# Second attention: q, k and v projections as products of 64 rows in two banks of PSUM

## What is computed

```python
xh = x.reshape(b, c, h, he).transpose(0, 2, 1, 3)         # 16 heads of 16 numbers
qkv = jnp.einsum('bhce,ef->bhcf', xh, Wqkv) + bqkv         # the same 16 x 48 weights for every head
q, k, v = jnp.split(qkv, 3, axis=-1)
att = jnp.einsum('bhqe,bhke->bhqk', q, k) / jnp.sqrt(jnp.float32(he))
mask = jnp.tril(jnp.ones((c, c), dtype=att.dtype), k=-1)
att = jax.nn.softmax(att * mask, axis=-1)
out = jnp.einsum('bhqk,bhke->bhqe', att, v)
out = out.transpose(0, 2, 1, 3).reshape(b, c, d) @ Wr + br
```

## Time and profile before

| what | value |
| --- | --- |
| three runs | 2794.32, 2801.05, 2802.73 us; median 2801.05 |
| profiled execution, its time | 2797.78 us |
| profiled execution, its span | 2796.0 us |
| TensorE, busy share of the span | 94% |
| VectorE | 82% |
| ScalarE | 74% |
| GpSimd | 65% |

### The profile page before, as it was taken

One profiled execution on the slowest core, in us unless ns is written; L12 is line 12 of the kernel. 1 busy time (PEld: TensorE's weight loads), 2 busy tenths in 40 slices (PEclk: granted clock), 3 DMA queues, 4 the chain that ended last, 5 costly groups with the idle time before them and its releaser, 6 DMA issues. The chain is left out here.

```text
span 2796.0 us, 75274 instructions
## 1 busy us (share of the span) xinstructions
PE 2615.3 (94%) x27044; PEld 1818.8 (65%) x27044; DVE 2280.6 (82%) x6931; ACT 2078.2 (74%) x3782; POOL 1811.9 (65%) x3152
## 2 busy tenths in 40 slices
PE   5999999999999999997889789999999999699999
PEld 3677777777777777775333257777777777466766
DVE  5999999999999999986655468888888888488998
ACT  4998899999998999895333257667677776478886
POOL 3767666777667766774421157677777767588885
PEclk8999999999999999999899889999999999899999
DMA  4334433444334433441000166655556664000001
GB/s 116 68 62 77 79 61 62 74 80 79 61 64 80 73 61 62 72 72 47 10 0 1 32 106 105 105 96 104 97 101 97 104 99 71 1 16 24 24 24 39
DMA packets 110387, 182.21 MB, mean 65 GB/s; under 512 B 27008, under 2 KB 96384, under 8 KB 97920
## 3 DMA queue, kind: packets, MB, share of 16 engines
q1 hardware_dynamic: 106560, 176.61, 34.7%
q10 hardware_dynamic: 3456, 0.79, 0.2%
HBM read 116.25 MB, written 60.29 MB: 63 GB/s over the span
## 5 line engine op out<-in xcount | busy, mean ns | idle before, releaser
L808 POOL TENSOR_TENSOR ratio_scores<-ratio_scores,ratio_max_cols 128x512 f32<-128x512 f32 (+3 forms) x1024 | 726.1, 726 | 319.3 <-DVE ratio_max_cols L718 316.9
L1328 DVE CUSTOM_DVE_ANT_0 zeroed_unused<-bank,zeroed_drop 128x512 bf16<-128x512 f32 (+3 forms) x1024 | 440.0, 484 | 121.1 <-PE bank L198 120.9
L198 PE MATMUL bank<-ratio_k_stack,ratio_q_stack 102*128 102x512 bf16 (+7 forms) x2048 | 506.3, 303 | 33.4 <-DVE ratio_max_cols L718 17.5
L718 DVE CUSTOM_DVE_ANT_0 ratio_scores<-bank,ratio_scores 128x512 f32<-128x512 f32 (+3 forms) x1024 | 472.4, 489 | 22.2
L1216 ACT ACTIVATE zeroed_prob<-bank 128x512 f32<-128x512 f32 x640 | 370.1, 593 | 161.2 <-PE bank L1103 160.3
L580 ACT ACTIVATE ratio_prob<-bank 128x512 f32<-128x512 f32 x640 | 378.4, 592 | 105.5 <-PE bank L494 102.7
L708 DVE TENSOR_TENSOR ratio_scores<-bank,ratio_inverse 128x512 f32<-128x512 f32 x640 | 435.9, 681 | 16.8 <-PE bank L198 9.6
L491 PE MATMUL bank<-const_f_sb,ratio_scores 128*128 128x128 f32 x2560 | 409.9, 274 | 0.9 <-ACT ratio_prob L580 0.9
L569 ACT ACTIVATE ratio_inverse<-bank 128x512 f32<-128x512 f32 x640 | 381.1, 596 | 12.7 <-PE bank L201 12.6
L573 ACT ACTIVATE ratio_inverse<-ratio_inverse 128x1024 f32<-128x1024 f32 x320 | 338.6, 1058 | 10.1
L1446 POOL TENSOR_SCALAR_AFFINE_SELECT zeroed_prob<-zeroed_prob 128x256 f32<-128x256 f32 (+1 forms) x640 | 227.7, 361 | 178.0 <-ACT zeroed_prob L1216 172.2
(11 more groups left out here) (178 smaller groups left out, 5412.6 us busy)
## 6 DMA issues: line engine op xcount, KB each, us to landing
ratio_q_stack<-ratio_parts_q SPq DMA_DIRECT2D x186, 128.0 KB
ratio_k_stack<-ratio_parts_k SPq DMA_DIRECT2D x186, 128.0 KB
zeroed_q_stack<-zeroed_parts_q SPq DMA_DIRECT2D x186, 128.0 KB, 4.7
zeroed_k_stack<-zeroed_parts_k SPq DMA_DIRECT2D x186, 128.0 KB, 7.7
ratio_parts_q<-ratio_parts SPq DMA_DIRECT2D x96, 128.0 KB
ratio_parts_k<-ratio_parts SPq DMA_DIRECT2D x96, 128.0 KB
zeroed_parts_q<-zeroed_parts SPq DMA_DIRECT2D x96, 128.0 KB
zeroed_parts_k<-zeroed_parts SPq DMA_DIRECT2D x96, 128.0 KB
```

The lines of the kernel that those rows point to most:

```text
L198: i = e.matmul(bank[:, off:off + w], qs[0:rows, s, hh, ib * P:(ib + 1) * P], ks[0:rows, s, hh, 0:w], start=(k == 0), stop=mask is None, sk ...
L718: i = e.tensor_tensor_reduce(seg, dot_banks[n % 2][:, at], seg, 1.0, 0.0, ALU.mult, ALU.max, mx[:, pair % M_BUFS, c:c + 1])
L808: i = e.tensor_tensor(seg, seg, mx[:, pair % M_BUFS, c:c + 1].to_broadcast([P, w]), ALU.subtract)
L1328: i = e.tensor_tensor_reduce(unused[:, n % 2, at], bank[:, at], drop[:, L - (ib + 1) * P:L], 1.0, 0.0, ALU.add, ALU.max, mx[:, pair % FOLD ...
```

## The change

`project` and `values` use the fact that `w_in` is zero off the diagonal. Heads 0 to 3 (partitions 0 to 63) go to `prep_bank`, heads 4 to 7 to `o_bank`. For q and k each bank takes two products of 64 rows, 64 output columns and 256 tokens: the first 256 tokens land on partitions 0 to 63, the others on 64 to 127. The values take eight products of 64 rows, 128 tokens and 64 moving columns. ScalarE's first part, VectorE's rest and value addition then read two banks, each in an instruction of 256 columns. Since the parts lie otherwise in SBUF, each of them is sent in two transfers of 64 partitions.

The two uses of `o_bank` exclude each other. Projections and values wait for `o_group`, and `attend` waits for `prep_read`. Attends move from slots 7, 9, 11 to 8, 10, 11 (17, 19, 1 to 18, 0, 1), projections from slots 11 and 15 to 13 and 16, and for the second half of all from slots 1 and 5 to 0 and 2.

```diff
-Z_ATTEND_AT = (9, 11, 13)
+Z_ATTEND_AT = (10, 12, 13)
...
-Z_SPLIT_AT, Z_REST_AT, Z_MID_AT, Z_LO_AT = (11, 15), (12, 16), (13, 17), (14, 18)
+Z_REST_LAG, Z_MID_LAG, Z_LO_LAG = 1, 2, 3
...
-Z_SECOND_AT, Z_SECOND_REST_AT, Z_SECOND_MID_AT, Z_SECOND_LO_AT = (1, 5), (2, 6), (3, 7), (4, 8)
+Z_SECOND_AT = (0, 2)
...
+def split_at(n, halves):
+
+    half, at = divmod(n, HALF_UNITS)
+    if n in Z_SECOND_AT:
+        return 1, Z_SECOND_AT.index(n)
+    if half >= 0 and at in Z_SPLIT_AT and half + 2 < halves:
+        return half + 2, Z_SPLIT_AT.index(at)
     return None, None
...
+    two_banks = lambda n: max(prep[use] for slot, use in order if use[0] in "qkv" and slot <= n)
+    groups_before = lambda n: max(-((ZEROED_LAG + Z_ATTEND_AT[0] - n) // N_UNITS), 0)
...
+        quarters = ((prep_bank, slice(0, P // 2)), (o_bank, slice(P // 2, P)))
...
-            def project(half, side):
+            def project(half, side, n):
+
                 q.wait_ge(w.sem, w.loaded)
                 q.wait_ge(s["prep_read"], prep[sides[side], half] - 1)
-                e.matmul(prep_bank[:, :], w.w_in[:, side, :], xnT[:, half % 2, :], start=True, stop=True).then_inc(s["prep_filled"])
-
-            def values(half):
+                q.wait_ge(s["o_group"], groups_before(n))
+                for bank, heads in quarters:
+                    for k in range(2):
+                        i = e.matmul(bank[k * 64:(k + 1) * 64, 0:L // 2], w.w_in[heads, side, heads],
+                                     xnT[heads, half % 2, k * L // 2:(k + 1) * L // 2], start=True, stop=True, skip_group_check=True)
+                i.then_inc(s["prep_filled"])
+
+            def values(half, n):
                 q.wait_ge(s["prep_read"], prep["v", half] - 1)
+                q.wait_ge(s["o_group"], groups_before(n))
                 for t in range(T):
-                    i = e.matmul(prep_bank[:, t * P:(t + 1) * P], xnT[:, half % 2, t * P:(t + 1) * P], w.w_in[:, 2, :],
-                                 start=True, stop=True)
+                    for bank, heads in quarters:
+                        i = e.matmul(bank[:, t * 64:(t + 1) * 64], xnT[heads, half % 2, t * P:(t + 1) * P], w.w_in[heads, 2, heads],
+                                     start=True, stop=True, skip_group_check=True)
                 i.then_inc(s["prep_filled"])
...
                     q.wait_ge(s["o_group"], g)
+                    q.wait_ge(s["prep_read"], two_banks(n))
                     attend(e, g, part, o_bank, values_ones, prob, FOLD_PROBS, STACKS).then_inc(s["attended"])
...
-                e.activation(parts[:, side, 0, :], prep_bank[:, :], ACT.Identity, bias=w.bias_qk[:, side:side + 1]).then_inc(s["hi"])
+                for k, (bank, _) in enumerate(quarters):
+                    i = e.activation(parts[:, side, 0, k * L // 2:(k + 1) * L // 2], bank[:, 0:L // 2], ACT.Identity,
+                                     bias=w.bias_qk[:, side:side + 1])
+                i.then_inc(s["hi"])
...
-                e.scalar_tensor_tensor(out=rest[:, :], in0=prep_bank[:, :], scalar=w.bias_qk[:, side:side + 1],
-                                       in1=parts[:, side, 0, :], op0=ALU.add, op1=ALU.subtract).then_inc(s["prep_read"])
+                for k, (bank, _) in enumerate(quarters):
+                    cols = slice(k * L // 2, (k + 1) * L // 2)
+                    i = e.scalar_tensor_tensor(out=rest[:, cols], in0=bank[:, 0:L // 2], scalar=w.bias_qk[:, side:side + 1],
+                                               in1=parts[:, side, 0, cols], op0=ALU.add, op1=ALU.subtract)
+                i.then_inc(s["prep_read"])
...
-                    e.dma_start(part_dram[side][half % 2][part].rearrange("d h t -> h d t"),
-                                parts[:, side, part, :]).then_inc(s[f"parts_{sides[side]}"], 16)
+                    for k in range(2):
+                        to = part_dram[side][half % 2][part][:, :, k * L // 2:(k + 1) * L // 2]
+                        e.dma_start(to.rearrange("d (m h) t -> h d m t", m=2),
+                                    parts[k * 64:(k + 1) * 64, side, part, :]).then_inc(s[f"parts_{sides[side]}"], 16)
```

More of the change, by code:

```diff
@@ L1131, in project_row, with prepare @@
                 i.then_inc(s["post_filled"])
-            def prepare(half, at):
+            def prepare(n):
+                half, at = divmod(n, HALF_UNITS)
+                split, side = split_at(n, halves)
+                if split is not None:
+                    project(split, side, n)
                 if half + 1 < halves and at == Z_VALUES_AT:
-                    values(half + 1)
-                if half == 0 and at in Z_SECOND_AT:
-                    project(1, Z_SECOND_AT.index(at))
+                    values(half + 1, n)
                 if half % 2 == 0 and half + 2 < halves and at in Z_TURN_AT:
                     turn_x(half // 2 + 1, Z_TURN_AT.index(at))
-                if half + 2 < halves and at in Z_SPLIT_AT:
-                    project(half + 2, Z_SPLIT_AT.index(at))
                 if half + 1 < halves and at == Z_SUFFIX_AT:
@@ L1147, in pe @@
             turn_x(0, 1)
-            project(0, 0)
-            project(0, 1)
-            values(0)
+            project(0, 0, -1)
+            project(0, 1, -1)
+            values(0, -1)
             suffix_sums(0)
@@ L1156, in pe @@
                 if half < halves:
-                    prepare(half, at)
+                    prepare(n)
                 if n % PAIR_UNITS == TURN_MAX_SLOT and 0 < n // PAIR_UNITS <= total // PAIR_UNITS:
@@ L1250, in prepare @@
                         keep_x(half // 2 + 1, Z_TURN_AT.index(at))
-                if half == 0 and at in Z_SECOND_AT:
-                    split(1, Z_SECOND_AT.index(at))
-                if half == 0 and at in Z_SECOND_MID_AT:
-                    second_part(1, Z_SECOND_MID_AT.index(at))
-                if half + 2 < halves and at in Z_SPLIT_AT:
-                    split(half + 2, Z_SPLIT_AT.index(at))
-                if half + 2 < halves and at in Z_MID_AT:
-                    second_part(half + 2, Z_MID_AT.index(at))
                 if half + 1 < halves and at == Z_SUFFIX_AT:
@@ L1278, in act @@
                     fold(n // PAIR_UNITS - 2)
+                split_half, side = split_at(n, halves)
+                if split_half is not None:
+                    split(split_half, side)
+                split_half, side = split_at(n - Z_MID_LAG, halves)
+                if split_half is not None:
+                    second_part(split_half, side)
                 if half < halves:
@@ L1358, in prepare @@
                     values(half + 1)
-                if half == 0 and at in Z_SECOND_REST_AT:
-                    split(1, Z_SECOND_REST_AT.index(at))
                 if half % 2 == 0 and half + 2 < halves:
@@ L1363, in prepare @@
                         normal(half // 2 + 1, Z_XN_AT.index(at))
-                if half + 2 < halves and at in Z_REST_AT:
-                    split(half + 2, Z_REST_AT.index(at))
             normal(0, 0)
@@ L1377, in dve @@
                     maxima(n)
+                split_half, side = split_at(n - Z_REST_LAG, halves)
+                if split_half is not None:
+                    split(split_half, side)
                 if half < halves:
@@ L1448, in prepare @@
             def prepare(half, at):
-                if half == 0 and at in Z_SECOND_LO_AT:
-                    split(1, Z_SECOND_LO_AT.index(at))
-                if half + 2 < halves and at in Z_LO_AT:
-                    split(half + 2, Z_LO_AT.index(at))
                 if half + 1 < halves and at == Z_TAILS_AT:
@@ L1470, in pool @@
                     split_maxima(pair - 1)
+                split_half, side = split_at(n - Z_LO_LAG, halves)
+                if split_half is not None:
+                    split(split_half, side)
                 if half < halves:
```

39 lines of the change are left out of this document (22 added, 17 removed).

## The result

The changed kernel takes 2949.9 us (median of four runs, 2946.55 to 2951.86) against 2798.8 before, 1.054 times (95%: 1.052 to 1.056): 151 us slower. That is outside the range, on the side that was forecast.

The account below looks back on a forecast made before the run. TensorE's work and waits were taken as the bound. Slot 18's wait (29 x 1.1 = 32), moved attends (30 x 0.7 = 21) and start (2) add 55 us to 2797.8, plus 1: 2854 us; range 2788 to 2888.

Parts of the forecast that it names:

- Products and evictions: Each half: projection 0.66 us, 0.25 less; values 0.2 us more on TensorE; each split eviction pair 0.15 us more.
- The new wait: Attend of slot 18 waits for VectorE's rest of k, making slot 19's dots 1.1 us later in 29 halves.
- The moved attends: Second attend, slot 9 to 10: dots of slot 10 wait for slot 7's maxima, 0.7 us in 30 halves.
- The moved slots: Projections in later slots: k's in 16, its rest in 17, priced within the 1.1 us wait at slot 18.
- Transfers: Six sends a side instead of three: hidden by TensorE's work in steady state, 2 us later at the stage's start.
- The first: Rival: the change delivers its saving, VectorE and ScalarE being done when the attend comes; 2783 to 2791 us, chance 0.20.
- The second: Rival: waits cost a third of the price, as TensorE's old waits for ScalarE go away; 2795 to 2825 us, chance 0.17.
- The third: Rival: sends on four engines become the bound, 3 to 9 us in a half; 2890 to 3060 us, chance 0.08.
- the idle at slot 18: Sign: TensorE idle 1 us or more before the first attend of slot 18, released by VectorE's rest.
- the dots released by the maxima: Sign: in slot 10, TensorE's dots wait until VectorE's maxima release them.
- VectorE below 81%: Sign: VectorE's busy share in the second attention falls below 81%.
- a half of 26.6: Sign: a half of the second attention lasts about 26.6 us instead of 24.8.

Follow-up runs that it names:

- One product: Changed kernel with the old products, evictions and sends, all changed waits and slots, and a rest buffer for each side: 2884.4 us, ratio 1.029.
- two rests: Changed kernel with a rest buffer of its own for each side, k's in the buffer of the normalized rows: 2877.4 us, ratio 1.027.
- Warm wait: Changed kernel with the dots of slot 19 computed eight extra times, unread, ahead of the attend of slot 18: 2919.7 us, ratio 1.043.
- Third part first: Changed kernel, one rest buffer, with q's third part ahead of the split of the maxima on GpSimd: 2915.2 us, ratio 1.041.
- both moves: Kernel before with projections in slots 13 and 16 and attends in 10, 12, 13 of their group's lag, nothing else: 2859.6 us, ratio 1.021.

## Why the prediction was right in sign and wrong in size

- **Products and evictions: right.** A projection takes 0.60 us (predicted 0.66), the values 1.04 (16 instructions from 1936.22, the next shift at 1937.26; predicted 1.1), a pair of rests 0.88 instead of 0.75 (0.15 predicted). One product against four with two rests shows a saving of 0.5 us a half with the values' loss of 0.24 in it, so 0.7 for both projections, where I had 0.5.
- **The new wait: the failed step.** "The work that VectorE has between the maxima of slot 12 and the k rest is what it was": the work is, the waits are not. I put in gaps of 0.2 and 0.1 us. I had moved q's third part to slot 16 on GpSimd and k's rest to 17 on VectorE, and did not ask what holds the `rest` buffer between them; before, k's rest stood two slots behind q's third part, and its idle time was nearly all for ScalarE, none for GpSimd. That gap is 1.19 us, and lifting it is worth 72 us. From the maxima of slot 12 to the attend I had 7.0 us (1913.66 to 1920.7). The changed kernel takes 8.70 (1917.52 to 1926.22), with two rests 7.33 (1916.99 to 1924.32). So the rest of this chain was nearly as forecast, and with the wait lifted the time, 2877 us, lies inside the stated range.
- **The clock: not in the sum.** I took all of TensorE's durations at full clock. The fall shown above lasts 3.4 us at half clock, which costs 1.7 us; my estimate for the 18 halves with one is 31 us. Warm wait, without any, is 30 us faster. The clock is a part of the 72, not beside it: two rests take 37 us of idle from the attends (66.6 to 29.5 us, 29 waits each, 1500 to 2560 us) and all the falls, 37 + 31 = 68. Third part first takes 26 us of idle (66.6 to 40.7) and three of the falls, 26 + 5 = 31 of its 35.
- **The moved attends: a term mis-sized.** 0.7 us for the second was right (+0.7 alone); the first (+0.5) was missing. Together they cost 32 us where I had 21.
- **The moved slots.** I had priced the late rest only through the attend. Alone it costs 30 us at the suffix products. In the changed kernel it is no extra term, since the attend's wait stands ahead of them; both moves give 58 us, and the shared bank with its long wait 70 more, partly by the clock.
- **Transfers.** Hidden in the steady state: right (k's gathers land in 7.4 us by the page, 7.7 in the earlier trace rows), and the share of 0.27 is the one named. The start was mis-sized: 6 to 10 us by the sends alone, 8.9 in the changed kernel, where I had 2 and a bound of 5.
- **Rivals.** The first asked that k's rest be read before TensorE comes to the attend; the attend waited for it in 29 halves. The second's trade of waits was not there: TensorE's waits for exponentials grew from 11.0 us in 34 to 20.5 us in 57 (1500 to 2560 us). The third (sends as bound) had the time within its range, for the wrong reason: a gather holds no slot 0 in the steady state. The signs fared alike: the idle at slot 18, the dots released by the maxima and VectorE below 81% were seen, a half of 26.6 was not.

The sum by runs, 149 us over the 2801 of their kernel before: both moves 58, the shared bank's waits with the old products 70, and 21 for the products, evictions and sends by four. These 21 are known to about 8 us either way. Other kernels price the sends at 10 and the values at 7.5 of them, which leaves some 4 for the projections, where I had counted on a saving of 16. So the saving does not come through in this chain: the attends wait 66.6 us for the rest with four products and 57.6 with one (1500 to 2560 us). That the split rest and first part, which lie in the chain, are the reason is argued and not shown by a run; nor is it shown that the projections are a loss by themselves. Why the first attend's move costs 0.5 us stays open as well.

## What to carry to other kernels

When a step moves to a later slot, list for every buffer of its chain who wrote and who read it last, on every engine, at the new distance; a distance of two slots that never waited became a distance of one that waited in each half. When a chain shares a bank with work of the bounding engine, price that engine's idle twice, once as time and once as the clock that it may lose. And weigh a saving on the bounding engine against the moves that it asks for: here 0.3 us on each of 64 projections, some 20 us, were bought with moves that cost 58.

## What the runs showed of the hardware

TensorE's granted clock has two levels here, 1.00 and 0.50 (2.4 and 1.2 GHz). In the changed kernel it was still 1.00 while TensorE stood, up to 1926.2 us. It fell some 0.4 us after the attend had begun, was 0.50 from 1926.6 to 1930.0 us, and then 1.00 again. The attend took 1.67 us instead of 1.08 and the first suffix products 1.90 instead of 1.02.

The length of the idle time alone does not say whether the clock falls. Behind 2.31 to 2.40 us it fell in 18 of 24 halves of the changed kernel. With third part first, where most attends stood 1.15 to 1.60 us, it fell in 15 of 28. With two rests, at most 1.2 us, it fell in none of 29, and in warm wait, at most 0.7 us, in none of 28. What decides between halves with the same idle time is not shown.

Eight repeated dots that nobody reads, 1.9 us of work in the wait, made the kernel 30 us faster.
